# A graph attention kernel whose neighbour mask is made by ScalarE's Relu in place of VectorE

## The reference, cut to what matters

```python
h = (x @ W).reshape(n, heads, out_c)
al_s = jnp.einsum('nhc,hc->nh', h, a_src)
al_d = jnp.einsum('nhc,hc->nh', h, a_dst)
e = jax.nn.leaky_relu(al_s[src] + al_d[dst], NEG_SLOPE)
m = jax.ops.segment_max(e, dst, num_segments=n)
ex = jnp.exp(e - m[dst])
```

## Time and profile before

| | |
|---|---|
| median of 3 runs | 1525.05 us |
| lowest and highest | 1524.69 and 1527.17 us |
| span of the profiled execution | 1518.7 us |
| median less this span | 6.35 us |
| TensorE busy | 1360.8 us, 90% |
| VectorE busy | 1160.0 us, 76% |
| ScalarE busy | 737.2 us, 49% |
| GpSimd busy | 505.1 us, 33% |

### The profile page before, as it was taken

How to read it: one execution, slowest core, us unless ns; L and a number is a source line. 1 busy time by engine, 2 the same in 40 slices (tenths; PEclk the granted TensorE clock), 3 DMA queues, 4 the chain that set the end, 5 groups by cost and what they waited for, 6 DMA issues and landing times. The chain is left out here.

```text
span 1518.7 us, 31335 instructions
## 1 busy us (share of the span) xinstructions
PE 1360.8 (90%) x7728; PEld 1135.4 (75%) x7739; DVE 1160.0 (76%) x1823; ACT 737.2 (49%) x1171; POOL 505.1 (33%) x557
## 2 busy tenths in 40 slices
PE   6888888888778889889977999999999999999995
PEld 4555656733223348889967999999999999999995
DVE  6499999899999988858878477555565655888882
ACT  3556465255555553422224455444454544666662
POOL 1000000003333410032324555555465555555563
PEclk9999999799999999999977999999999999999998
DMA  6300001041222214233566987867778876799963
GB/s 233 138 18 9 18 28 61 18 179 61 73 95 63 78 44 141 63 105 106 127 166 216 269 223 204 186 166 170 171 193 205 203 191 159 210 271 273 254 135 49
DMA packets 102255, 211.68 MB, mean 139 GB/s; under 512 B 19318, under 2 KB 58486, under 8 KB 102082
## 3 DMA queue, kind: packets, MB, share of 16 engines
q1 hardware_dynamic: 79186, 142.06, 28.7%
q0 software_dynamic: 22240, 66.69, 22.0%
q10 hardware_dynamic: 784, 2.36, 0.4%
HBM read 164.14 MB, written 54.93 MB: 144 GB/s over the span
## 5 line engine op out<-in xcount | busy, mean ns | idle before, releaser
L992 PE MATMUL ps_o<-prob,h_head 128*97 128x512 f32 (+1 forms) x480 | 187.7, 528 | 51.5 <-DVE prob L934 51.5
L2070 POOL DMA_INDIRECT out_nodes<-y,to_index x92 | 160.1, 1740 | 133.9 <-issue 73.5
L2387 PE MATMUL ps_h<-e_hi,e_xt_hi 128*128 (+1 forms) x546 | 192.6, 353 | 6.3 <-ACT e_xt_hi L2189 3.6
L992 PEld LDWEIGHTS ps_o<-prob,h_head 128*97 128x97 f32 x480 | 73.2, 164 | 165.4 <-issue 89.7
L2372 PE MATMUL ps_y<-e_hi,e_ht_hi 128*128 (+1 forms) x546 | 191.6, 351 | 3.6 <-DVE e_ht_lo L2305 2.2
L2387 PE MATMUL ps_h<-e_lo,e_xt_hi 128*128 (+1 forms) x546 | 184.7, 338 | 0.0
L2372 PE MATMUL ps_y<-e_hi,e_ht_lo 128*128 (+1 forms) x546 | 183.6, 336 | 0.0
L2372 PE MATMUL ps_y<-e_lo,e_ht_hi 128*128 (+1 forms) x546 | 183.5, 336 | 0.0
L2254 DVE TENSOR_TENSOR e_lo<-raw,e_hi (+1 forms) x189 | 175.6, 950 | 7.3 <-ACT e_hi L2197 6.7
L2207 ACT ACTIVATE y<-ps_y,gate 128x768 f32 (+1 forms) x91 | 82.2, 903 | 192.4 <-PE ps_y L2372 124.2
L826 ACT ACTIVATE score<-score,al_col 128x1250 f32<-128x1250 f32 x80 | 106.0, 1335 | 98.4 <-DVE score L877 98.4
(11 more groups left out here) (357 smaller groups left out, 3053.0 us busy)
## 6 DMA issues: line engine op xcount, KB each, us to landing
raw<-in_ew SPq DMA_DIRECT2D x192, 384.0 KB, 5.7
w_room<-rel_dram SPq DMA_DIRECT2D x14, 640.0 KB, 4.6
b_all<-in_eb SPq DMA_DIRECT2D x32, 192.0 KB
al_src<-al_dram SPq DMA_DIRECT2D x1, 5000.0 KB, 14.6
xs<-in_x SPq DMA_DIRECT2D x5, 768.0 KB, 12.5
x_in_t<-in_x SPq DMA_DIRECT2D x10, 384.0 KB, 3.7
out_nodes<-x SPq DMA_DIRECT2D x10, 384.0 KB, 4.2
table<-xf SPq DMA_DIRECT2D x10, 384.0 KB, 2.7
```

Of the source, the lines that this page charges most:

```text
L992: turn = nc.tensor.matmul(ps_o[u][0:C1 + 1, c, 0:WID[c]], h_head[:, u, t, :], prob[:, t % 2, 512 * c:512 * c + WID[c]], start=(t == 0), st ...
L2070: nc.gpsimd.indirect_dma_start(out, bass.IndirectOffsetOnAxis(to_index[:, w:w + 1], 0), y[:, w, :], None, bounds_check=NP - 1, oob_is_err= ...
L2387: nc.tensor.matmul(ps_h[:, 0:HID], xt_hi[:, c, :], b[:, bass.ds(e % 2, 1), c * HID:(c + 1) * HID] .rearrange("p o m -> p (o m)"), start=(c ...
```

## The change

ScalarE makes the mask, with one Relu of `counts` scaled by -1e30 and a bias of 1e30, which is kept in a new column `far`: the result is 1e30 where there is no edge and 0 where there is one. The sign is turned, so the maxima of both layers subtract the mask, and the row of `al_s` becomes the first operand. GpSimd sets `far` before its other memset, and ScalarE waits for both. ScalarE makes the mask of tile t - 1 behind the turned counts of that tile; the mask of tile 9 it makes in front of its two copies of `ps_h`. The waits on `counts_kept`, `mask_out` and `maxed` go with the mask.

```diff
+        far = sb("far", [P, 1])
...
             @block.gpsimd
             def _(pool):
+                nc.gpsimd.memset(far[:, :], -NOT_A_NEIGHBOUR).then_inc(ones_set, 1)
                 nc.gpsimd.memset(s.h_ext[:, :, :, C1:C1 + 1], 1.0).then_inc(ones_set, 1)
-                pool.wait_ge(ones_set, 1)
+                pool.wait_ge(ones_set, 2)
...
+                def mark_far(t):
+
+                    act.wait_ge(counts_kept, t + 1)
+                    if t:
+                        act.wait_ge(mask_out, 16 * t)
+                        act.wait_ge(maxed, t * H1)
+                    nc.scalar.activation(mask[:, :], counts[:, :], ACT.Relu, bias=far[:, 0:1],
+                                         scale=NOT_A_NEIGHBOUR).then_inc(mask_made, 1)
+
                 act.sem_inc(dst_made, 2)
+                act.wait_ge(ones_set, 2)
                 for t in range(NT):
...
                     if t:
                         keep_turned(t - 1)
+                        mark_far(t - 1)
+                        act.wait_ge(turned, t)
                         act.wait_ge(mask_made, t)
-                        act.wait_ge(turned, t)
                     act.wait_ge(counted, t + 1)
...
                     act.wait_ge(h_summed, t + 1)
                     for half in range(2):
+                        if t == NT - 1 and not half:
+                            mark_far(t)
                         last = nc.scalar.activation(
...
                 def largest(t):
 
-                    dve.wait_ge(counts_kept, t + 1)
-                    if t:
-                        dve.wait_ge(mask_out, 16 * t)
-                        dve.wait_ge(maxed, t * H1)
-                    nc.vector.tensor_scalar(mask[:, :], counts[:, :], 0.0, NOT_A_NEIGHBOUR,
-                                            ALU.is_equal, ALU.mult).then_inc(mask_made, 1)
                     dve.wait_ge(al_in, 16)
                     dve.wait_ge(mask_made, t + 1)
...
                         nc.vector.tensor_tensor_reduce(
-                            junk(t, h), mask[:, 0:N].rearrange("p (a b) -> p a b", b=ROOM),
-                            al_src[:, h, :].rearrange("p (a b) -> p a b", b=ROOM), 1.0,
-                            2.0 * NOT_A_NEIGHBOUR, ALU.add, ALU.max, s.al_max[:, t, h:h + 1]).then_inc(maxed, 1)
+                            junk(t, h), al_src[:, h, :].rearrange("p (a b) -> p a b", b=ROOM),
+                            mask[:, 0:N].rearrange("p (a b) -> p a b", b=ROOM), 1.0,
+                            2.0 * NOT_A_NEIGHBOUR, ALU.subtract, ALU.max, s.al_max[:, t, h:h + 1]).then_inc(maxed, 1)
...
-                    nc.vector.tensor_tensor_reduce(junk[:, t % 2, :], mask[:, t % MASKS, :], everywhere, 1.0,
-                                                   2.0 * NOT_A_NEIGHBOUR, ALU.add, ALU.max,
+                    nc.vector.tensor_tensor_reduce(junk[:, t % 2, :], everywhere, mask[:, t % MASKS, :], 1.0,
+                                                   2.0 * NOT_A_NEIGHBOUR, ALU.subtract, ALU.max,
                                                    best[:, t:t + 1]).then_inc(maxed, 1)
```

## The result

| | before | changed |
|---|---|---|
| median of 7 runs | 1526.73 us | 1531.36 us |
| lowest and highest | 1521.13 and 1529.00 | 1528.74 and 1534.27 |
| span of the profiled execution | 1518.7 | 1528.4 (its own time 1531.36) |
| stage, from its first load to the next stage's first copy | 243.33 | 251.40 |

The changed kernel is slower: ratio 1.0038, 95% interval 1.0025 to 1.0051, that is 3.8 to 7.8 us; the medians lie 4.6 us apart. 7.9 us were forecast, just above the upper end of the interval. The time forecast was 1533.0 us, from the median of the first three runs before; the seven runs have 1526.73. The stage itself, read in one profile of each kernel, grew by 8.1 us. The stage length used from here on runs from SP's load of `al_src` (50.13 us before, 50.00 after) to ScalarE's `h_head` copy behind the barrier (293.46 and 301.40).

The account below looks back on a forecast made before the run. A ring of TensorE and ScalarE was taken to bound the edge-counting loop, with VectorE following. Loop 0, start 0.4 and end 7.5 us gave 7.9 us on 1525.05, so 1533.0 us, range 1527.0 to 1536.0.

Parts of the forecast that it names:

- A ring of TensorE and ScalarE: Edge-counting loop: counts, features, ScalarE's copy and first one-hot, TensorE again; VectorE runs beside it; loop change nothing.
- VectorE's saving turns into a wait: Tiles 0 to 7: VectorE has 0.82 us less to do but begins its maxima 0.6 us later, waiting for ScalarE.
- The rival in which the later maxima delay eight tiles: Loop: VectorE's mask chain bounds, each of eight tiles loses 0.6 us, 4.8 + 7.9 = 12.7, 1537.8 us; chance 0.06.
- One sign that I had named as wrong: Tile starts: TensorE waiting over 0.4 us for one_src would show VectorE is in the ring.
- the slack of 0.8 us: Tile start: VectorE's first one-hot pair is ready some 0.8 us before TensorE wants it.
- the tile that I took for all: The one tile whose timeline stood for eight, with TensorE starting at 144.86 us.
- the 0.6 us: Tiles 0 to 7: later start of VectorE's maxima, 132.54 against 131.94 us, claimed to lie within the 0.8 us slack.
- The rival of the other side: Edge-counting stage: VectorE bounds it and its ten masks come off, 8.2 us faster, 1516.9 us; chance 0.04.
- The start, 0.4 us: Stage start: ScalarE waits for two GpSimd memsets, making ScalarE and TensorE 0.4 us late, bounds 0 and 0.6.
- The last tile: Tile 9's mask waits for the 72nd maximum before the ps_h copies, delaying 96 small matmuls; loss 7.5 us.
- the clock has fallen for the whole block, 0.60 against 0.15: Last 96 matmuls: all at clock 0.50, 15.6 us, forecast chance 0.60; rival's clock falls within the block, 1529.9, chance 0.15.
- The sum: Whole kernel: 0 loop, 0.4 start, 7.5 end, 7.9 us; added to median 1525.05, keeping 6.35 us between span and median.

Follow-up runs that it names:

- the sign alone: Kernel before, mask still on VectorE, with the mask's sign turned and the maxima of both layers with swapped operands and a subtraction; ratio 1.0001, stage 243.58 us.
- the wait alone: Kernel before, VectorE making all masks, plus ScalarE waiting for the 72nd maximum before the last two ps_h copies; ratio 1.0022, stage 245.65 us.
- its second profile: The changed kernel run and profiled again, unchanged; ratio 1.0037 to the kernel before, stage 250.86 us.
- the three others that keep its loop: Changed kernel with tile 9's mask behind the ps_h copies (1.0009), with that mask in its own place (1.0004), or with 38 TensorE transposes in the wait (1.0007).
- the moved split: Feature split moved behind the turned counts, in the kernel before (ratio 0.9990) and in the changed kernel with its order mended (0.9980).
- the last pair of kernels: Split moved and loop bounds read early, in the kernel before (ratio 0.9949, 236.92 us) and in the changed kernel with order mended (0.9942, 235.92 us).
- the pair in which the split is moved: Only the split moved in the kernel before (0.9990); the changed kernel with order mended and split moved (0.9980).
- the mask in its own place: Changed kernel with tile 9's mask written to a free one-hot slot, same position, without the wait for the 72nd maximum; ratio 1.0004, stage 244.77 us.
- The kernel with the filler: Changed kernel with 38 transposes on TensorE before its wait for the ps_h copies; ratio 1.0007, stage 247.13 us.
- bounds alone: Kernel before with only the next tile's edge bounds read early, the split left between tiles; ratio 0.9993, stage 242.69 us.
- all twelve comparisons in the table: The changed kernel, its repeat and ten other variants, each against runs of the kernel before; ratios from 0.9942 to 1.0038.

## Why the prediction was right, point by point

- *A ring of TensorE and ScalarE bounds the loop, and VectorE follows.* Right. The gap at the tile start reacted to what ScalarE does there, by 0.65 to 0.73 us a tile, and not to who makes the mask. From TensorE's first product of tile 0 to that of tile 9 the kernel before took 207.18 us, with the sign alone 207.53 and with the wait alone 207.74; the changed one took 208.01 and, in its second profile, 207.38, and the three others that keep its loop 207.35, 207.66 and 206.51. So the loop costs nothing that these profiles can tell. One part of my picture, on which the forecast didn't rest, was wrong: the gap held the reading of the loop bounds beside the copies, split and one-hot, and I hadn't seen it, so the moved split gave next to nothing.
- *VectorE's saving turns into a wait.* Right. That the first maximum came within 0.01 us (132.55 against 132.54) is luck in the last digit, since the two profiles' stages begin 0.13 us apart. The rival in which the later maxima delay eight tiles, by 4.8 us, falls with the loop's length. One sign that I had named as wrong did come, three waits for `one_src` of 1.88 us at a tile's start; the end times above show that VectorE wasn't what they waited for. But the slack of 0.8 us was misread. I took it up to TensorE's start, which comes 0.4 us after the first `one_dst` is ready. Against that `one_dst`, VectorE's first pair was ahead by 0.45 us in the tile that I took for all, and by 0.9 to 1.1 us at the seven others; in the changed kernel it is ahead by 0.3 to 0.9 us at six starts and behind by 0.1 and 0.16 us at two, where TensorE's wait was still 1.88 and 1.87 us. So the 0.6 us were covered, but only just. The Trainium skill's advice to keep a relu off ScalarE (ScalarE: Activation LUTs, "Rules for kernel authors") holds for the price of one mask here, 0.82 against 1.35 us, and said nothing of the time, as neither lay on the path in the loop. In the last pair of kernels the one with ScalarE's masks was 1.0 us shorter in the stage, of which 0.5 us lie between two profiles of one kernel.
- *The rival of the other side, VectorE bounds the stage:* falls with the same rows, and with the pair in which the split is moved: with ScalarE's masks, made early, the stage took 242.25 us, with VectorE's 242.62. Taking eight masks off VectorE would have given 6.6 us if VectorE were the bound.
- *The start, 0.4 us.* Too much. The two memsets overlapped, 50.00 and 50.04 us, and the first product came 4.06 us after the stage's start where it was 3.90: 0.2 us, of 0.4.
- *The last tile.* Right in each step and within 0.8 us: Relu at 282.44 us (281.72 forecast), block at 284.71 (284.1), 15.47 us long (15.6), stage ended by TensorE. Which of the wait and the work costs was only argued; the mask in its own place (6.6 us back) shows it is the wait. The wait alone costs 2.3 us in the kernel before; in the changed one the copies come another 3.1 us later, read from the stage's start (1.8 for the later 72nd maximum, 1.3 for the Relu behind the wait), and the block takes 2.7 us more, at the lower clock. The three make 8.1. That the clock has fallen for the whole block, 0.60 against 0.15, was right as well: it fell at 284.73 us with the block at 284.71, and in the second profile 0.6 us ahead of it. The kernel with the filler shows the cause.
- *The sum.* 7.9 us forecast; the stage grew by 8.1 and by 7.5 us in two profiles of the changed kernel, but the times by 4.6 and 5.9 us at the median, with intervals that end at 7.8 us. That 8.1 is so near 7.9 is in part luck: it holds 0.8 us of a loop that the other profiles call chance, 0.2 for the start and 7.1 for the end. The step that was off is the one that set the sum against the median as if the rest stood still, and took the 6.35 us between span and median as fixed. In the runs on record an execution's own time is 1.9 to 3.7 us above its span, so a span of 1518.7 us belongs to an execution of some 1521 us (an estimate), as fast as the fastest of the seven, 1521.13. From the `h_head` copy to the end, the profiles took between 1225.2 us (the kernel before) and 1230.8 us (sign alone) with hardly any change there. So a difference of 8 us in one stage lies beside one of some 5 us in the rest that goes by chance, and the profile of before had the shortest rest of those read. Whether the stage of the kernel before is often longer than in its profile wasn't seen: its two nearest kin, sign alone and bounds alone, took 243.58 and 242.69 us. Over all twelve comparisons in the table, the change in time (by the ratio) lies on average 1.1 us below the change in the stage, which hints, and no more, that the stage in the profile of before is about 1 us short. Why a part of the 8 us is missing from the medians stays open.

## What to carry to other kernels

When work moves to another engine, its waits move too: look at what is queued behind them there, above all in the last turn of a loop, where the order differs and nothing follows to hide it. If two things fill the same gap, removing either gives next to nothing (0.6 to 1.1 us here, against 6.4 and 7.4 for both); read the engine's queue (register loads, branches) beside its instructions before the gap is put down to the work that is seen in it. Check a wait's label against the end times of what is waited for: here three labels changed with no change in time, and named an engine that had been ready 0.5 us before the other.

## What the runs showed of the hardware

Reading two loop bounds into registers keeps ScalarE's queue for about 1.1 us (141.4 to 142.5). In that time its engine works off what was issued before, the copies and the split, and stands idle once that is done (0.53 us with the split gone). Read early, in front of the wait for the features, the bounds cost nothing that shows: the stage took 242.69 us against 243.33. And 4.6 us of nothing on TensorE set the 96 small matmuls that follow to 0.161 us each (15.47 us), where 4.31 us of transposes in that time brought them to 0.133 (12.73 us); 1.21 and 2.09 us of nothing did no such harm (12.61 and 12.80 us). In the eleven profiles with at most 2.09 us of nothing ahead of the block, the granted clock fell 3.0 to 5.4 us after the block had begun, which by itself moves the block between 10.7 and 12.8 us; in the two with 4.62 and 4.69 us it had fallen when the block began or 0.02 us later.
